# GpSimd's scatter of a chunk placed ahead of the second half-gather of an older chunk, with a third result buffer

## What is computed

```python
def _L0_xattn_ref(q, k, v):               # per token: 16 heads x 8
    scores = jnp.einsum('bsqd,bskd->bsqk', qh, kh) / math.sqrt(hd)
    scores = jnp.where(mask, scores, NEG_INF)
    out = jnp.einsum('bsqk,bskd->bsqd', softmax(scores), vh)
def _L0_ffn_ref(x, ...):
    shared_out = (silu(xf @ sw1) * (xf @ sw3)) @ sw2
    rw, sel = jax.lax.top_k(xf @ router_w.T + experts_bias, 2)
    cw = (one_hot(sel, 8) * softmax(rw)[..., None]).sum(axis=1)
    moe_out = jnp.einsum('te,teh,ehd->td', cw, silu(g) * u, w2)
    return moe_out + shared_out
x = x + tanh(g_xattn[0]) * xattn(layernorm(x), ctx_1024, ctx_1024)
x = x + tanh(g_ffn[0]) * ffn(layernorm(x), ...)
```

## Time and profile before

| | |
|---|---|
| median of 3 runs | 791.93 us |
| the profiled execution: its time / its span | 795.51 us / 793.6 us |
| mean granted TensorE clock | 0.878 |
| TensorE matmul busy | 547.0 us (69%) |
| VectorE busy | 481.2 us (61%) |
| GpSimd busy | 442.4 us (56%) |
| ScalarE busy | 275.9 us (35%) |

### The profile page before, as it was taken

How to read it: one execution, slowest core, us unless ns; L and a number is a source line. 1 busy time by engine, 2 the same in 40 slices (tenths; PEclk the granted TensorE clock), 3 DMA queues, 4 the chain that set the end, 5 groups by cost and what they waited for, 6 DMA issues and landing times. The chain is left out here.

```text
span 793.6 us, 12846 instructions
## 1 busy us (share of the span) xinstructions
PE 547.0 (69%) x3769; PEld 480.5 (61%) x3769; DVE 481.2 (61%) x963; ACT 275.9 (35%) x658; POOL 442.4 (56%) x458
## 2 busy tenths in 40 slices
PE   0063281989697896887488959793889799758900
PEld 0032150878597776875388749772879599748900
DVE  3977993779757984797268947893557244212200
ACT  2021320266136622662066304640275116213400
POOL 4102256035663886388547855687647567648166
PEclk9997566899989998999699979997899999969955
DMA  7901001374266526752457436741657267548633
GB/s 257 173 8 53 1 11 57 133 226 138 65 174 217 147 87 162 238 153 78 140 154 226 117 97 167 239 113 61 179 180 197 86 161 207 157 126 219 184 63 56
DMA packets 113184, 109.30 MB, mean 138 GB/s; under 512 B 10328, under 2 KB 84320, under 8 KB 113120
## 3 DMA queue, kind: packets, MB, share of 16 engines
q1 hardware_dynamic: 90304, 91.64, 37.5%
q0 software_dynamic: 22528, 16.86, 12.1%
q10 hardware_dynamic: 288, 0.00, 0.0%
HBM read 32.48 MB, written 27.75 MB: 76 GB/s over the span
## 5 line engine op out<-in xcount | busy, mean ns | idle before, releaser
L499 POOL DMA_INDIRECT xo<-rows_out,idx x128 | 209.2, 1634 | 39.4 <-issue 38.8
L875 PE MATMUL ps_g<-xrT,wq 128*128 128x128 f32 x1472 | 183.9, 278 | 5.3 <-DMA wq<-w 5.3
L875 PEld LDWEIGHTS ps_g<-xrT,wq 128*128 128x128 f32 x1472 | 175.3, 194 | 8.2 <-DMA wq<-w 5.8
L666 DVE TENSOR_TENSOR eo<-sil,ps_g 128x512 f32<-128x512 f32 x124 | 84.6, 683 | 156.2 <-ACT sil L755 119.6
L820 PE MATMUL ps_o<-pv,ident 128*128 128x320 f32 (+15 forms) x512 | 146.9, 425 | 44.2 <-DVE pv L580 37.0
L481 POOL DMA_INDIRECT rows_in<-xn,idx x128 | 144.2, 1126 | 38.5 <-issue 38.5
L900 PE MATMUL ps_y<-w2s,eo 128*128 (+1 forms) x992 | 142.8, 290 | 23.2 <-ACT yr L773 14.0
L900 PEld LDWEIGHTS ps_y<-w2s,eo 128*128 128x128 f32 x992 | 130.4, 203 | 34.5 <-issue 32.7
L755 ACT ACTIVATE sil<-ps_g 128x512 f32<-128x512 f32 x124 | 74.1, 597 | 202.0 <-PE ps_g L875 86.1
L820 PEld LDWEIGHTS ps_o<-pv,ident 128*128 128x128 f32 x512 | 86.9, 201 | 72.4 <-issue 62.2
L445 POOL TENSOR_TENSOR msum<-stats 128x8 f32<-128x8 f32 x16 | 10.1, 634 | 168.2 <-DVE stats L533 168.2
(11 more groups left out here) (83 smaller groups left out, 376.4 us busy)
## 6 DMA issues: line engine op xcount, KB each, us to landing
wq<-w SPq DMA_DIRECT2D x184, 256.0 KB
rows_out<-yr SPq DMA_DIRECT2D x88, 128.0 KB
xr<-rows_in SPq DMA_DIRECT2D x40, 258.0 KB
xt<-in_x SPq DMA_DIRECT2D x8, 512.0 KB, 4.2
ct<-in_ctx SPq DMA_DIRECT2D x8, 512.0 KB, 5.9
out<-xo SPq DMA_DIRECT2D x7, 512.0 KB
rows_in<-empty SPq DMA_DIRECT2D x2, 1483.5 KB, 20.8
w<-in_L_ffn_w SPq DMA_DIRECT2D x2, 1024.0 KB, 11.4
```

The lines of the kernel that those rows point to most:

```text
L499: pool.indirect_dma_start(xo[:, par, t], None, rows_out[par], bass.IndirectOffsetOnAxis(ap=idx[:, c % 3, k * T + t:k * T + t + 1], axis=0) ...
L666: nc.vector.tensor_tensor(eo[:, p % 2].rearrange("p c a r -> p (c a r)"), sil[:, p % 2], ps_g[p % 2][:, 1].rearrange("p c r -> p (c r)"), ...
L875: last = nc.tensor.matmul(into[:, q // HC, q % HC, a * P:(a + 1) * P], wq[:, i % WR, q * P:(q + 1) * P], xrT[:, p % 3, a * P:(a + 1) * P], ...
```

## The change

In every step GpSimd's `scatter(m-1)` moves ahead of `gather(m-3, 1)`. `xo` has three buffers in place of two, and VectorE's first write to `xo` of a chunk waits for the result of three chunks back (two before).

```diff
-        xo = sb("xo", [P, 2, T, D])
+        xo = sb("xo", [P, 3, T, D])
...
-                sp.dma_start(tokens(o_f, c * TOKEN_WORDS)[:, ts], xo[:, c % 2, ts]).then_inc(s["out"], 16)
+                sp.dma_start(tokens(o_f, c * TOKEN_WORDS)[:, ts], xo[:, c % 3, ts]).then_inc(s["out"], 16)
...
-                        xo[:, par, t], None, rows_out[par],
+                        xo[:, c % 3, t], None, rows_out[par],
...
+                scatter(m - 1)
                 if m >= 3:
                     gather(m - 3, 1)
-                scatter(m - 1)
                 if m >= 2:
                     gather(m - 2, 0)
...
-                    need(dve, s["out"], 16 * c)
+                    need(dve, s["out"], 16 * (c - 1) if c > 2 else 0)
...
-                nc.vector.scalar_tensor_tensor(xo[:, c % 2, t:t + w],
+                nc.vector.scalar_tensor_tensor(xo[:, c % 3, t:t + w],
```

## The result

The changed kernel takes 866.54 us (median of 4 runs, 865.05 to 868.7) against 791.93 us for the kernel before (median of 3 runs timed beside it): a ratio of 1.0944, 95% interval 1.0914 to 1.0974. It is slower by 74.6 us. The forecast was 871 us, range 848 to 888. (A fourth run of the kernel before took 1958.68 us and is left out.)

A forecast was written before the change was run, and what follows sets the result against it. TensorE's stall on each step's first xr read was taken to bound the kernel. Later reads over six steps (69.25 us) plus slower landing (9.6) gave 78.9 us, added to the median 791.93: 871 us, range 848 to 888.

The forecast's parts named there:

- What bounds it: TensorE's stall on each step's first xr read: 16.27 us in step 4, 8.22 in step 3, every microsecond the program's.
- The scatter moves up: GpSimd: scatter ends 24.06 us after pos, 9.55 us earlier in step 4, 4.09 in step 3; unchanged in step 7.
- The rival in which it is starved under VectorE's work: GpSimd's scatter at its slow DMA's pace, 8.4 us more in four steps, 905 us; chance of 888 to 930: 0.09.
- The half-gather moves back and SyncE's list does the rest: Half-gather ends 15.08 us after the scatter, result 1.79 later; xr read behind it, 17.88 or 18.48 us after scatter end.
- The faster rival: SyncE's queue does not hold the read back; only the earlier scatter counts, 27.3 us less, 764.7 us; chance 0.03.
- The mis-sized term: xr read's landing behind the result's 512 KB on the same queue: 1.6 us in each of six steps, 9.6 us.
- the sum: Lateness of the first xr read or transpose over steps 3 to 8, without the landing: 69.25 us.
- The end: Program end: GpSimd waits 20.1 us for the last stores, so TensorE's lateness reaches the end whole.
- Step 8: First transpose 12.08 us later, counted from 709.28, when TensorE reached it; 16.5 us if counted whole.
- The signs: Changed profile: TensorE's xr waits near 160 us, 21 to 25 in steps 3 to 7; step 4 read 42 after pos.

The follow-up runs named there:

- e1: Changed kernel with SyncE issuing the result in slot 30 instead of slot 17, behind the first reads of rows_in; 776.37 us, ratio 0.9801 to the kernel before.
- e4: Changed kernel with SyncE still waiting for the half-gathers in slot 17 but issuing the result in slot 22, behind the first xr read; 861.0 us, ratio 1.0882.
- e2: Changed kernel with GpSimd's old order (half-gather ahead of scatter), three xo buffers, and the result in slot 30; 793.93 us, ratio 1.0029.
- e9: Kernel before with only three xo buffers and VectorE's relaxed wait, GpSimd's old order, result in slot 17; 791.88 us, ratio 0.9979.

## Why the prediction was right

**What bounds it.** That TensorE's stall on the first `xr` read decides, and that every microsecond of the read is one of the program, held: 73.0 us at the six transposes, 70.6 in the span.

**The scatter moves up.** Forecast 24.06 us from `pos` to its end, measured 24.34 to 24.75 in steps 3 to 6; in steps 7 and 8 unchanged. The rival in which it is starved under VectorE's work did not come: from its first DMA to the end of its last the scatter took 23.56 us in step 4, where VectorE was busy for 22.2 of the 24.7 us from `pos`, and 20.28 us in step 8, where VectorE was busy for 5.3 of 21.5 us. (Two slips of the rivals are small: 24.06 less the start is 23.05 us and not 23.4, which gives 906 and not 905, and 27.3 us less than 791.93 is 764.6.)

**The half-gather moves back and SyncE's list does the rest.** Forecast 15.08 us for it, measured 14.85 in step 4 (387.36 to 402.21); 1.79 us to the result, measured 1.79; the read 41.9 us after `pos` in step 4 and 42.5 in step 3, measured 42.31 and 42.87. The faster rival turned on this one place; e1 is that case made real, and its 776 us against the rival's 765 also shows what the rival left out, GpSimd's lateness. The prediction had read GpSimd's time to spare in step 4 alone, 10.43 us; in step 3 it was 6.68.

**The mis-sized term** is the landing of the read behind the result's data: 1.6 us a step, 9.6 in all, "nearest to what the paired loads show". From issue to transpose it is 3.38 to 3.84 us after, against some 3.1 before: about 0.5 us a step, 3 us in all. Without that error the sum would have been 69.25 + 3.0 = 72.3 us against 73.0 measured. The paired loads both go from HBM into SBUF; the result goes the other way, and in the changed kernel its 512 KB land in 2.7 us by the median, where a load of the same size needs 4.3. That this is why the term was too large is not shown. The rule of the Trainium skill that I had set beside it ("DMA: Bandwidth & Descriptors", "Queues, rings and completion order") would allow the full 1.6 us. In step 4 the two landed in the order that it speaks of, but the result at 406.8 (2.8 us after its issue) and the read at 408.6 (3.7 us after), 1.8 us apart, so it held nothing back there. e4 measures 0.1 to 0.6 us for the landing in the six steps, and the measurement decides.

**The end.** GpSimd's wait for the last stores was to carry TensorE's lateness to the end whole: it is 18.7 us at the longest, 20.1 before. The span grew by 2.4 us less than the six transposes moved; this lies partly ahead of step 3, where `pos` comes 1.64 us sooner after that of step 2 (79.46 against 81.10). In that stretch the first matmuls behind the stall are shorter in this execution: the first eight into `ps_g` took 1.89 us at a granted clock of 1.00, and 2.94 before, at 0.64. It is no effect of the change, which begins in step 3.

**What was luck.** Step 8 of the profiled execution, from which the forecast counted, was a long one: its first transpose came 30.43 us after `pos`, but 26.17 and 26.02 us in e2 and e9, which have GpSimd's old order and run as fast as the kernel before. Set against e9's profile, step 8 loses 16.8 us (the prediction's bound for it was 16.5, its term 12.1), and the span grows by 74.7 us, which is the 74.6 between the medians. So against the medians the landing was 6.5 us too large and step 8 some 4.4 us too small, and the two errors partly cancel. Whether the third buffer or chance shortens step 8 in e2 and e9 is not settled.

**The signs.** TensorE's wait on the reads was put at 160 us and is 173.7, since in step 8 it now counts 30.3 us, of which 11.1 stood under another wait before (L900 on `yr`), and the forecast had 13.7 there. The stalls of steps 3 to 7 were put at 21 to 25 us and are 21.8 to 24.4. In step 4 `idx` starts 0.43 us after `pos`, as foretold, and the first scatter DMA at 1.17.

## What to carry to other kernels

Before an instruction is moved behind another on one engine, look for who waits for it on the issuing queues, and what stands behind that wait: here the result of a chunk three steps old, which could wait for the end of the step, held the read that every engine needed. A wait in an in-order list should stand behind everything that is wanted sooner; the two moves belong together, and the second (one number) turned 9% slower into 2% faster. Then ask what the engine whose work was moved has to do next: cutting the half-gather, so that it fills the wait for `pos` and does not run into the next layer norm, was worth 6 to 9 us more (from 776.4 to between 767.7 and 770.8).

## What was not expected of the hardware

In steps 7 and 8 of the kernel before, ScalarE waits without a named releaser, 23.2 us in three waits at L755 and 4.6 in two at L773, where the result's 512 KB are issued under a running scatter. With three buffers and the result still in slot 17 (e9) such waits are still there, in part:

```profile
ACT sil L755 <- remote: 11.6, 2, 7.9
ACT yr L773 <- remote: 4.4, 1, 4.4
```

All of these lie in step 8: 15.9 us, where the kernel before had 16.8. In step 7 the kernel before had 11.0 us and e9 has none, although its result leaves under the scatter there too. With the same order on GpSimd and the result in slot 30 (e2) there is none in either step, nor in the changed kernel, where the result leaves after the scatter. So in step 8 they are not the old wait on the buffer; for step 7 that is not excluded. They appear only in kernels that issue the result during the scatter, but not in every such step: in steps 3 to 6 the result of the kernel before also leaves within the scatter, 0.6 to 1.3 us behind its first DMA, and shows no such wait. What they cost is small, since the stall on the read follows anyway (e2 and e9 are no faster by their medians), and what ScalarE waits for stays open.
